# Adding the expert's second bias outside TensorE in the routed feed-forward stage

## The reference, cut to what matters

```python
logits = xt @ Wg.T
top1 = jnp.argmax(logits, axis=-1)
xhat = (xt - mu) * jax.lax.rsqrt(var + LN_EPS)
# for each expert:
h = jax.nn.gelu((xhat * s_e + b_e) @ w1 + bb1, approximate=False)
out = h @ w2 + bb2
mask = (top1 == eid)[:, None].astype(out.dtype)
y = y + mask * out
# and at the end
x = x + y
```

## Time and profile before

| | us |
|---|---|
| median of 3 runs | 2977.99 |
| lowest and highest | 2976.95 and 2979.15 |
| the profiled execution | 2978.57 |
| span of its instructions | 2976.8 |

### The profile page before, as it was taken

One profiled execution on the slowest core, in us unless ns is written; L12 is line 12 of the kernel. 1 busy time (PEld: TensorE's weight loads), 2 busy tenths in 40 slices (PEclk: granted clock), 3 DMA queues, 4 the chain that ended last, 5 costly groups with the idle time before them and its releaser, 6 DMA issues. The chain is left out here.

```text
span 2976.8 us, 43504 instructions
## 1 busy us (share of the span) xinstructions
PE 2708.4 (91%) x15650; PEld 2298.4 (77%) x15650; DVE 2081.7 (70%) x4205; ACT 1573.6 (53%) x3080; POOL 1542.0 (52%) x1155
## 2 busy tenths in 40 slices
PE   6799999978668699999999999999999999799688
PEld 5688877755424598998989989989899898677576
DVE  4677777742438577777777777777777777577656
ACT  2343443431205477777777777777777677111175
POOL 2355445330002466666666666666666666365555
PEclk9899999987776799999999999999999999899899
DMA  5211222114329523223332232333322313577475
GB/s 184 56 52 55 56 55 55 54 36 165 113 83 368 178 72 101 69 73 101 79 106 69 72 101 69 79 95 78 108 69 72 99 45 126 177 269 261 160 279 190
DMA packets 184384, 337.21 MB, mean 113 GB/s; under 512 B 52360, under 2 KB 58507, under 8 KB 177101
## 3 DMA queue, kind: packets, MB, share of 16 engines
q1 hardware_dynamic: 161937, 259.40, 29.5%
q0 software_dynamic: 11680, 45.02, 4.1%
q10 hardware_dynamic: 10560, 30.08, 2.6%
HBM read 166.39 MB, written 148.71 MB: 106 GB/s over the span
## 5 line engine op out<-in xcount | busy, mean ns | idle before, releaser
L1720 POOL TENSOR_SCALAR pa_Pr<-pa_Pr,pa_rs 128x590 f32<-128x590 f32 x512 | 902.7, 1768 | 549.7 <-DVE pa_rs L1951 549.5
L1955 DVE TENSOR_REDUCE pa_least<-pa_S 128x1 f32<-128x590 f32 x512 | 391.0, 764 | 209.4 <-PE pa_S L1785 207.1
L1907 DVE TENSOR_TENSOR pa_PTl<-pa_W,pa_PTh 128x512 fp32r<-128x512 f32 (+1 forms) x640 | 420.9, 683 | 30.2 <-ACT pa_PTh L1845 23.0
L1875 ACT ACTIVATE pa_Pr<-pa_S,pa_least 128x590 f32<-128x590 f32 x512 | 384.8, 752 | 81.7 <-DVE pa_least L1955 78.3
L1845 ACT ACTIVATE pa_PTh<-pa_W 128x512 fp32r<-128x512 f32 (+1 forms) x640 | 367.4, 596 | 83.1 <-PE pa_W L1796 63.7
L1796 PE MATMUL pa_W<-pa_ident,pa_Pr 128*128 128x128 f32 (+1 forms) x2560 | 367.0, 274 | 1.2 <-DVE pa_U L1907 0.6
L1796 PEld LDWEIGHTS pa_W<-pa_ident,pa_Pr 128*128 128x128 f32 (+1 forms) x2560 | 304.8, 142 | 25.6 <-POOL pa_Pr L1720 2.8
L1810 PE MATMUL pa_O<-pa_PTh,pa_V 128*128 128x512 f32 (+1 forms) x640 | 288.7, 451 | 18.2 <-DVE pa_PTl L1907 14.0
L1811 PE MATMUL pa_O<-pa_PTl,pa_V 128*128 128x512 f32 (+1 forms) x640 | 253.9, 397 | 0.0
L1783 PE MATMUL pa_S<-pa_U,pa_Qh 128*128 128x296 f32 (+1 forms) x1024 | 227.0, 303 | 0.2
L1785 PE MATMUL pa_S<-pa_Um,pa_Ql 128*128 128x296 f32 (+1 forms) x1024 | 223.2, 299 | 0.0
(11 more groups left out here) (469 smaller groups left out, 6786.5 us busy)
## 6 DMA issues: line engine op xcount, KB each, us to landing
xs_s<-pa_Ql SPq DMA_DIRECT2D x57, 576.0 KB
pa_Um<-pa_U SPq DMA_DIRECT2D x128, 147.5 KB
pa_Qh<-pa_Qh SPq DMA_DIRECT2D x128, 128.0 KB
o_s<-pa_O_hi SPq DMA_DIRECT2D x64, 256.0 KB, 2.0
o_s<-pa_O_lo SPq DMA_DIRECT2D x64, 256.0 KB, 2.3
Wkv_hi<-o_s SPq DMA_DIRECT2D x8, 2048.0 KB, 11.6
Wkv_lo<-o_s SPq DMA_DIRECT2D x8, 2048.0 KB, 17.1
z_s<-la_z_hi ACTq DMA_DIRECT2D x8, 1180.0 KB, 7.8
```

The lines of the kernel that those rows point to most:

```text
L1720: pool.tensor_scalar(p, p, rs[:, g % 2, t:t + 1], None, ALU.mult).then_inc(*pool_s.mark("probs", n))
L1875: act.activation(Pr[g % 2][:, t, :], scored[n % 2], ACT.Exp, scale=-1.0, bias=least[:, g % 2, t:t + 1], accum_out=rs[:, g % 2, t:t + 1]).t ...
L1907: dve.tensor_tensor(out, src, f32(hi_ap), ALU.subtract).then_inc(*dve_s.mark(*name))
L1955: dve.tensor_reduce(least[:, g % 2, t:t + 1], scored[n % 2], AX, ALU.min).then_inc(*dve_s.mark("least", n))
```

## The change

The product with `bias_rows` goes, with the matrix itself. The table `wt_s` now holds the whole float32 bias in every partition's row: one DRAM to DRAM DMA with a broadcast source writes it, in the place of three DMAs from SBUF, and the load of b2 into SBUF, its split by ScalarE and VectorE, and two memsets go. In the loop, the sum of the gathered residual and the bias is written to `Y4` ahead of the result: for the row groups j = 0 and 1 by GpSimd, for j = 2 and 3 by VectorE. `result` then adds the PSUM bank to `Y4` in place.

```diff
@@ SyncE, batch 0
-                    sp.wait_ge(small_cut, 2)
-                    sp.wait_ge(setup, 10)
-                    sp.dma_start(by_expert[2:P, :, B2:B2 + D], f32(h[1][0][2:P, :]).unsqueeze(1).to_broadcast([P - 2, E, D])).then_inc(table, 16)
-                    for x in range(2):
-                        sp.dma_start(wt_s.rearrange("(e p) w -> e p w", p=P)[:, x, B2:B2 + D], f32(h[0][x][0:E, :])).then_inc(table, 16)
+                    sp.dma_start(wt_s.rearrange("(e p) w -> e p w", p=P)[:, :, B2:B2 + D],
+                                 a["L1_ffn_b2"].unsqueeze(1).to_broadcast([E, P, D])).then_inc(table, 16)
@@ GpSimd
+            def with_bias(i, j):
+                if j == 0:
+                    pool.wait_ge(rows_in[i % NF], 16 * (i // NF + 1))
+                    pool.wait_ge(wt_in[i % NW], 16 * (i // NW + 1))
+                    pool.wait_ge(free[i % 4], sends(i % 4) + 16 * NT * (i // 4))
+                pool.tensor_tensor(Y4[i % 4][:, j, :], F4[i % NF][:, j, 0:D], f32(Wt[i % NW][:, B2:B2 + D]), ALU.add).then_inc(*pool_s.mark("x+b2", i, j))
+
+            for j in range(2):
+                with_bias(0, j)
             for i in range(TILES):
...
                 if tile(i + NF):
                     fetch_rows(i + NF)
+                if tile(i + 1):
+                    for j in range(2):
+                        with_bias(i + 1, j)
@@ TensorE, second_product
-                pe.matmul(ps[:, :], bias_rows[:, :], w[:, B2:B2 + D], start=True, stop=False)
                 pe.wait_ge(*dve_s.after("lo", i))
-                product(pe, ps[:, :], [z[:, j * P:(j + 1) * P] for z in h[i % 2]], [w[:, (2 + x) * D:(3 + x) * D] for x in range(2)], False, True)\
+                product(pe, ps[:, :], [z[:, j * P:(j + 1) * P] for z in h[i % 2]], [w[:, (2 + x) * D:(3 + x) * D] for x in range(2)], True, True)\
@@ VectorE
-                dve.wait_ge(*pe_s.after("y", i, j))
-                dve.tensor_tensor(Y4[i % 4][:, j, :], bank_of["y", i, j][:, :], F4[n][:, j, 0:D], ALU.add)\
+                dve.wait_ge(*pe_s.after("y", i, j))
+                dve.wait_ge(*(pool_s if j < 2 else dve_s).after("x+b2", i, j))
+                dve.tensor_tensor(Y4[i % 4][:, j, :], bank_of["y", i, j][:, :], Y4[i % 4][:, j, :], ALU.add)\
+                   .then_inc(*dve_s.mark("free", "y", i, j))
+
+            def with_bias(i, j):
+                if j == 2:
+                    dve.wait_ge(rows_in[i % NF], 16 * (i // NF + 1))
+                    dve.wait_ge(wt_in[i % NW], 16 * (i // NW + 1))
                     dve.wait_ge(free[i % 4], sends(i % 4) + 16 * NT * (i // 4))
+                dve.tensor_tensor(Y4[i % 4][:, j, :], F4[i % NF][:, j, 0:D], f32(Wt[i % NW][:, B2:B2 + D]), ALU.add).then_inc(*dve_s.mark("x+b2", i, j))
...
                     if j == 0 and tile(i):
                         low(i)
+                    if j >= 2 and tile(i):
+                        with_bias(i, j)
```

More of the change, by code:

```diff
@@ L2011, in build_experts @@
         tri, ones = sb("tri", [P, P]), sb("ones", [P, P])
-        bias_rows = sb("bias_rows", [P, P], F32R)
         Wout, o = read_out_tiles(Wq, Wkv, T)
@@ L2026, in build_experts @@
         LT = sb("LT", [E, T])
-        b2_raw = LT
         L, top = sb("L", [P, NT, E]), sb("top", [P, NT, E])
@@ L2063, in build_experts @@
         smalls = [(gain[:, :], a["L1_ffn_ln_scale"]), (shift[:, :], a["L1_ffn_ln_bias"]), (b1[:, :], a["L1_ffn_b1"]),
-                  (Wg_raw[:, :, :], chunks(a["Wg_T"])), (b2_raw[:, :], a["L1_ffn_b2"]),
+                  (Wg_raw[:, :, :], chunks(a["Wg_T"])),
                   (g_bc[:, :], a["L1_xattn_ln_o_g"].partition_broadcast(P)),
@@ L2164, in _ @@
             iota(pcol, [[1, 1]], 1)
-            pool.memset(f32(h[1][0][:, :]), 0.0).then_inc(setup, 1)
             pool.memset(ones[:, :], 1.0).then_inc(setup, 1)
-            pool.memset(f32(bias_rows[:, :]), 0.0).then_inc(setup, 1)
             pool.memset(cum[0][:, 0, :], 0.0).then_inc(setup, 1)
@@ L2170, in _ @@
             pool.wait_ge(pads, 4)
-            pool.wait_ge(setup, 13)
+            pool.wait_ge(setup, 11)
             def scale(n):
@@ L2260, in _ @@
                 pool.wait_ge(stored[n], 32 * NCH // 2)
-            pool.wait_ge(table, 64)
+            pool.wait_ge(table, 32)
             pool.wait_ge(*dve_s.after("wsrc"))
@@ L2306, in gate_logits @@
                 ps = claim(pe, "LT", b)
-                pe.wait_ge(small_cut, 2)
+                pe.wait_ge(small_cut, 1)
                 for c in range(C):
@@ L2321, in ranks @@
                 ps = claim(pe, "rank", b)
-                pe.wait_ge(consts, 2)
+                pe.wait_ge(consts, 1)
                 pe.wait_ge(*dve_s.after("hot", b))
@@ L2365, in second_product @@
                 ps = claim(pe, "y", i, j)
-                pe.matmul(ps[:, :], bias_rows[:, :], w[:, B2:B2 + D], start=True, stop=False)
                 pe.wait_ge(*dve_s.after("lo", i))
-                product(pe, ps[:, :], [z[:, j * P:(j + 1) * P] for z in h[i % 2]], [w[:, (2 + x) * D:(3 + x) * D] for x in range(2)], False, True)\
+                product(pe, ps[:, :], [z[:, j * P:(j + 1) * P] for z in h[i % 2]], [w[:, (2 + x) * D:(3 + x) * D] for x in range(2)], True, True)\
                     .then_inc(*pe_s.mark("y", i, j))
-            pe.wait_ge(setup, 13)
+            pe.wait_ge(setup, 11)
             for b in range(B + 2):
@@ L2420, in _ @@
             act.activation(Wg[0][:, :, :], Wg_raw[:, :, :], ACT.Copy).then_inc(*act_s.mark("Wg hi"))
-            act.activation(h[0][0][0:E, :], b2_raw[:, :], ACT.Copy).then_inc(*act_s.mark("b2 hi"))
             for b in range(B + 1):
@@ L2590, in constants @@
                 dve.tensor_scalar(tri[:, :], prow[:, :], pcol[:, 0:1], None, ALU.is_gt).then_inc(consts, 1)
-                dve.memset(f32(bias_rows[0:2, :]), 1.0).then_inc(consts, 1)
                 step("no later", dve.tensor_tensor, ee[1][:, :, :], eight[:, :].unsqueeze(1).to_broadcast([P, E, E]),
@@ L2599, in constants @@
                     step(("base", rows_of), dve.scalar_tensor_tensor, t[:, :], region[:, :], float(rows_of), t[:, :], ALU.mult, ALU.add)
-            dve.wait_ge(setup, 13)
+            dve.wait_ge(setup, 11)
             constants()
@@ L2604, in _ @@
             dve.tensor_tensor(Wg[1][:, :, :], Wg_raw[:, :, :], f32(Wg[0][:, :, :]), ALU.subtract).then_inc(small_cut, 1)
-            dve.wait_ge(*act_s.after("b2 hi"))
-            dve.tensor_tensor(h[0][1][0:E, :], b2_raw[:, :], f32(h[0][0][0:E, :]), ALU.subtract).then_inc(small_cut, 1)
             dve.wait_ge(small, 16 * len(smalls))
@@ L2646, in result @@
                        .then_inc(*dve_s.mark("tok", i))
+                dve.wait_ge(*pe_s.after("y", i, j))
[6 more added lines that the diff above has]
+                    dve.wait_ge(wt_in[i % NW], 16 * (i // NW + 1))
                     dve.wait_ge(free[i % 4], sends(i % 4) + 16 * NT * (i // 4))
-                dve.wait_ge(*pe_s.after("y", i, j))
-                dve.tensor_tensor(Y4[i % 4][:, j, :], bank_of["y", i, j][:, :], F4[n][:, j, 0:D], ALU.add)\
-                   .then_inc(*dve_s.mark("free", "y", i, j))
+                dve.tensor_tensor(Y4[i % 4][:, j, :], F4[i % NF][:, j, 0:D], f32(Wt[i % NW][:, B2:B2 + D]), ALU.add).then_inc(*dve_s.mark("x+b2", i, j))
             def low(i):
```

## The result

| | kernel before | kernel after |
|---|---|---|
| median of 5 runs | 2977.99 us (2968.93 to 2979.15) | 3017.23 us (3014.18 to 3021.34) |
| ratio | | 1.0138, 95% interval 1.0126 to 1.015: **slower by 39 us** |
| span of the profiled execution | 2976.8 | 3019.6 |
| predicted | | 3016 (2998 to 3029) |

A forecast was written before the change was run, and what follows sets the result against it. TensorE bounded the kernel at 8.27 us a tile. With GpSimd as new bound, rounds up to 11.7 us put the span at 3015.8, less 1.0 at the start, plus 1.8 outside: 3016.6, predicted as 3016 us (2998 to 3029).

The forecast's parts named there:

- The mechanism: Loop: GpSimd's DMAs and additions plus waits for VectorE's results make rounds of 11.7 us, TensorE idling; chance 0.70.
- the prediction's own signs: Wrong if GpSimd's additions clearly miss 1.26 us or overlap the DMA issue, or routing moves by more than 3 us.
- 11.3 without the block: Loop: round with both fetches is 11.3 us if `low` is not blocked by GpSimd's second addition, 11.7 if it is.
- The short rounds: Loop, late tiles with no fetch: rounds of 9.1 us, or 8.7 without the block of `low`.
- the two cases: Loop: `low` waits for GpSimd's second addition (rounds 11.7, 10.4, 9.1) or does not (11.3, 10.0, 8.7).
- The start of the stage: Routing part before the loop: 1.0 us gained by one load and steps fewer, 0 for SP's DMAs, about 6 lost if loads are delayed.
- VectorE's 6.8 us are below 7.33, so it does not bound: Loop: VectorE's own work with two additions is 6.8 us a tile, below TensorE's new period of 7.33.
- GpSimd alone: Rival, loop: GpSimd's own work alone bounds, VectorE never holds a scatter back; round 10.2 us, time 3000; chance 0.14.
- The clock: Rival, loop: idle TensorE falls to 1.2 GHz and is late in short rounds; +8 us, time 3024; chance 0.08.
- The additions fit into the time between DMAs: Rival, loop: GpSimd's additions cost nothing, scatters set the pace at 7.76 us; time 2968; chance 0.05.

The follow-up runs named there:

- e8: Kernel after with a product of zeros and the bias columns put back on TensorE in place of the bias product; ratio to kernel before 1.0131.
- e1: Kernel after with the DRAM to DRAM bias copy issued in batch 6 instead of batch 0; 3005.1 us, ratio to kernel before 1.0092.
- e2: Kernel after with the bias columns written from a zeroed SBUF tile instead of DRAM, bias left out of the result; ratio to kernel before 1.0113.
- e9: Kernel before with its three DMAs for the bias columns in batch 6 instead of batch 0; ratio to kernel before 0.9985.
- e3: Kernel after with all four additions of residual and bias on VectorE, none on GpSimd; 2998.6 us, ratio to kernel before 1.0067.
- e6: As e5, but VectorE's two additions left out, with the bias of these rows; ratio to kernel before 1.0045, on the chip with uneven rounds.
- e5: Kernel after with GpSimd's two additions for the next tile ahead of the two fetches instead of behind them; ratio to kernel before 1.0108.
- e10: Kernel after without any addition of the bias (left out of the result) and with the copy in batch 6; ratio to kernel before 0.9974.
- e7: As e3, but the four VectorE additions behind the tile's last transposed_lo, and the copy in batch 6; ratio to kernel before 0.9976.
- e11: The kernel of e7 run again on another chip; ratio to kernel before 1.0003.

## Why the prediction was right, step by step

**The mechanism** was right. GpSimd's additions close a round with its DMAs and with VectorE's results, TensorE idles in it, and taking the product away brings nothing (e8). In us after the end of GpSimd's first addition, T = 2902.60:

| | forecast | measured |
|---|---|---|
| scatters start | 1.7, 3.86, 5.15, 6.86 | 1.71, 3.65, 4.95, 6.61 |
| weights, rows | 8.14, 9.43 | 7.89, 9.18 |
| next addition starts, ends | 10.47, 11.7 | 10.22, 11.30 |

By the prediction's own signs it was not clean: it was to be wrong if the additions took clearly more or less than 1.26 us, and they took 1.08, or if the routing part moved by more than 3 us, and it moved by 4.9. The next paragraphs take both.

**The sizes that were off in the round** are two. GpSimd's addition takes 1.08 us, not 1.26. I took the four additions of 5.02 us, which write over one of their operands; the multiplications of the earlier trace rows were as near, with 2.05 for two. And `low` was held for 0.21 us, not 0.42: it was shown with 0.89 instead of 0.68 where I had said about 1.1. The cause is partly the same: the second addition ended sooner. Together they make 0.39 of the 0.4 us by which the round is shorter. That "11.3 without the block" came out exactly is chance: there is a block, and a shorter addition.

**The short rounds** came out longer than the 9.1 and 8.7 of the two cases: 9.55 and 10.16. In one of them the small `tok` operation stands beside GpSimd's additions and lasts 2.85 us instead of 0.2, and scatter 0 comes 0.85 later than in a long round. Timelines of POOL, then DVE, kernel after:

```profile
2986.66 2.15 POOL L2271 TENSOR_TENSOR ex_R<-Wkv_hi,ex_Wt 128x512 f32<-128x512 f32 x2
2990.30 0.99 POOL L2279 DMA_INDIRECT out<-ex_R,ex_tok  x1 [1.49 <-DVE ex_h_lo L2661]
```

```profile
2986.01 2.85 DVE L2645 TENSOR_SCALAR ex_tok<-Wkv_hi,ex_valid 128x4 uint32<-128x4 f32 x1
2988.77 0.68 DVE L2649 TENSOR_TENSOR ex_R<-ex_bank,ex_R 128x512 f32<-128x512 f32 x1
```

The `tok` operation is shown from 0.65 us before the additions, beside a scatter, until their end; why it was caught there and not in the other rounds stays open. In the other short round the last scatter starts after 2.39 us of idling for which the profile names no releaser; that stays open too. Timeline of POOL, kernel after:

```profile
2996.68 0.98 POOL L2279 DMA_INDIRECT out<-ex_R,ex_tok  x1 [2.39 <-issue]
```

e8 has both rounds too (9.56, 10.15), so neither is TensorE's. For the whole loop the errors left 36.5 us against a forecast of 39.2.

**The start of the stage** was the step that failed: forecast a gain of 1.0, measured a loss of 4.9. I had taken 0 for SP's exchange of three DMAs for one, with a bound of 6 if a copy that reads DRAM delayed the loads; that is what it does (e1, e2). The gain of 1.0 for the load and the steps that go can't be seen either: with the copies late both kernels take the same time here (e1, e9). The term with no row in the trace was set to the comfortable end of its bounds. That the total is 3017 against 3016 is luck in part. The span came out 4.8 us above the forecast of 3014.8: -2.7 in the loop, -0.1 before it, +5.9 in the routing part and +1.7 in code that the change doesn't touch. And the median of the runs lies 4.1 us below the profiled execution (3021.34), where I had reckoned with 0.6.

**"VectorE's 6.8 us are below 7.33, so it does not bound"** was wrong as an argument, though here it decided nothing. Its queue has the hole of 1.6 to 1.8 us seen in e3, so eleven operations need about 8.5 us: above 7.33, and about the old period. That is worked out from e3's rows; no run had these eleven operations alone.

**The rivals.** GpSimd alone (round 10.2) was not after's case but became true in e6, at 10.1. The clock fell to 0.93 in the stretch shown. No run holds it up or down, so that it cost nothing is argued, from twelve tiles whose first result follows GpSimd's addition and not TensorE, and from the room that e8 found. "The additions fit into the time between DMAs" is excluded by the rows above: none starts before its DMA has ended.

## What to carry to other kernels

Before work is moved to an engine, add up its period with the gaps between its instructions and the hole in which it waits for the others, and not its busy share: GpSimd at 74% busy had 0.5 us left in 8.27. If a second engine is right behind the bound, the gain stops there: 14 us of TensorE were worth at most 6.7. And a transfer that is put early in a queue is paid by the loads behind it; look at what the queue issues next, and move it to a stretch where nobody waits.

## What the runs showed of the hardware that I had not expected

**A DMA that GpSimd issues waits for a VectorE operation with two SBUF operands.** An indirect DMA that starts during one such operation takes up to 1.47 us instead of 0.98, during four in a row up to 2.35 in the rows shown (e5, e10, e7), and each of those shown ends within 0.04 us of 0.98 after VectorE's operation is over, with 0.60 us counted for one operation. Without the additions it is 0.99 to 1.01 (e6), though it starts there too while VectorE is busy, in operations with one operand in PSUM. The loops of all thirteen profiles agree: 122 of GpSimd's DMAs begin while VectorE is in an operation with two SBUF operands, and all of them end 0.9 to 1.06 us after the end of such an operation, counted as the start of VectorE's next one; none of the others lasts more than 1.1 us. With four additions in a row (e7, e11) nine DMAs were held only to the end of the addition in which they began, the others to the end of the fourth; what decides between the two stays open. In the prediction I took the opposite from the Trainium skill, SBUF — State Buffer, "Who interferes with whom", which infers that `tensor_tensor` leaves descriptor generation alone; the measurement decides against that inference, for this form of DMA at least. It had no weight in the forecast: in the kernel after only one DMA of the loop begins during such an operation. A `low` of 0.68 us beside a DMA did not speak for it: there VectorE began 0.38 us after the DMA, and neither was held. Beside GpSimd's additions, even a 128x4 operation of VectorE was held, 2.85 us instead of 0.2 (kernel after).

**One form of GpSimd addition has two prices.** 128x512 float32 additions took 1.08 us each in the loop, with a separate output, and 1.26 in the routing part, onto their own input. The multiplications of the earlier trace rows write over their input as well and take 1.03, so the output alone is not the reason; the cause of the 0.2 us stays open.
